# Image stage of a ViT tower with experts: attention heads doubled in round mode products, and a new order of the stage's work

## The chip, the cores and the metric

One core of a Trainium2 chip runs the whole program. The metric is the device time in microseconds (us) of one execution. Engines are named as in the profile: PE is TensorE's matmul and PEld its weight load, DVE is VectorE, ACT is ScalarE, POOL is GpSimd, SP is SyncE, which only issues DMAs here.

## The reference, cut to what matters

The input is 32 images of 3x256x256. Each becomes 256 tokens of 256 numbers (gray value, two Scharr filters, sum of absolute values), a class token is put in front, and an attention block and a layer of routed experts follow. The change touches the attention of the image rows alone:

```python
x_proj = jax.nn.silu(x @ W1 + b1)
u, v, q, k = jnp.split(x_proj, 4, axis=-1)          # 16 heads of 16 channels
scores = jnp.einsum("bqhd,bkhd->bhqk", qh, kh)
attn = jax.nn.silu(scores) / S
av = jnp.einsum("bhqk,bkhd->bqhd", attn, vh).reshape(B, S, D)
y = _layernorm(av * u, gamma, beta) @ W2 + b2
```

All data are float32.

## The kernel before, in words

The program has an image stage, a class stage, a router and an expert stage. The image stage is the subject here. It is one block in which each engine runs its own list of instructions; `steps` (L458) calls each engine's `body(n, r)` for n from -3 to 33, fully unrolled. A step works on five images at once, in a software pipeline: a = n+2 (edges, norm), b = n+1 (projections q, k, u, v), c = n (scores, silu, weighted sums), d = n-1 (gate, norm z, W2, residual h2, norm xf), e = n-2 (statistics of the rows and the router's first product). Gray images are made at gm = n+3 (L230 to L243). The order inside a step is written out by hand for each engine: PE at L619 to L669, ACT at L724 to L780, DVE at L844 to L913, POOL at L923, SP at L951. Engines meet in semaphores, so an instruction that waits holds all that is behind it on its engine.

PE's small results (all but scores and weighted sums) share two PSUM banks in turn: `UNITS` (L465) lists the 14 uses of a step, and `bank_free` (L473) makes a use wait until the use two places before it has been read (`READ`, L468). The four score products of an image write ps_s, which ACT must have read before the next (L557), and the weighted sums write ps_av.

Two kinds of matmul occur. Plain float32 operands (marked f32 and two records for each call in the trace): scores (`score`, L554), weighted sums (`weighted`, L565), edge filters (`conv`, L495), class scores (`cls_scores`, L536). Round mode operands (fp32r, one record for each call), where a value is split into a rounded part and a rest and multiplied three times (`mm3`, L198): the projections and W2. Heads have 16 channels, and a tile of the array has 32 rows. So ACT writes k twice in `silu_k` (L698), once with the odd heads' channels scaled to zero and once with the even heads' (four activations of 128x256), and a product over 32 rows of q and such a k gives one head. `score` issues 8 calls for each of its four parts, on four row tiles j.

```python
last = nc.tensor.matmul(ps_s[j // 2][:, j % 2, kt, :], k2[r % 2][32 * j:32 * j + 32, e, a, kt * 128:kt * 128 + 128],
                        q2[r % 2][32 * j:32 * j + 32, a, :], start=True, stop=True)
```

Of the kernel before, what the change touches and what calls it, by code (L numbers as in the profile page):

```python
# [18 lines left out]
P = 128  # L19
# [43 lines left out]
CE2 = CQM + 8  # L63
CLV = CE2 + 2
# [6 lines left out]
def constants(nb):  # L71
# [15 lines left out]
    for j in range(4):  # L87
        for par in range(2):
            c[32 * j + 16 * par:32 * j + 16 * par + 16, CQM + 4 * par + j] = 1
            c[32 * j + 16 * par:32 * j + 16 * par + 16, CE2 + par] = 1  # L90
# [26 lines left out]
def build(nc, x, cls_rows, w1, b1uv, b1qk, w2, b2, gb, taps, r1w, r1s, r1m, r1b, r2w, wexp, consts, out,  # L117
# [9 lines left out]
    with ctx:  # L127
# [42 lines left out]
        bk4 = s1("bk4", [P, 4])  # L170
# [97 lines left out]
        with nc.Block() as block:  # L268
# [42 lines left out]
            def _(dve):  # L311
# [48 lines left out]
                for a in range(2):  # L360
                    nc.vector.tensor_scalar(cw[:, a, :], cst[:, CMK:CMK + 32], qkcf[:, 2 + a, 0:1], None, ALU.mult)
                    nc.vector.tensor_scalar(cw[:, 2 + a, 0:8], cst[:, CQM:CQM + 8], qkcf[:, a, 0:1], None, ALU.mult)
                    nc.vector.tensor_scalar(bk4[:, 2 * a:2 * a + 2], b1qk_sb[:, 2:4], cst[:, CE2 + a:CE2 + a + 1], None, ALU.mult)
# [60 lines left out]
        q2 = [s1(f"q2{i}", [P, 2, D]) for i in range(2)]  # L424
        k2 = [s1(f"k2{i}", [P, 2, 2, D]) for i in range(2)]
# [15 lines left out]
        stat_a, ve_a, rs_a, xn_done, xt_ps, xt_hi, xt_done = (sem(n) for n in ("stat_a", "ve_a", "rs_a", "xn_done", "xt_ps", "xt_hi", "xt_done"))  # L441
        qk_ps, qk_act, uv_ps, uv_sum, uv_act = (sem(n) for n in ("qk_ps", "qk_act", "uv_ps", "uv_sum", "uv_act"))
# [15 lines left out]
        def steps(eng, body):  # L458


            for n in range(-3, NB + 2):
# [3 lines left out]
        UNITS = ["B0", "A0", "E", "D0", "D1", "G0", "B1", "D2", "A1", "D3", "B2", "B3", "B4", "D4"]  # L465
        LAG = {"E": 0, "G": -2, "D": -1, "B": 1, "A": 2}
# [4 lines left out]
                "B3": (uv_sum, 2, 1), "B4": (uv_sum, 2, 2), "D4": (xft_done, 1, 1)}  # L471
# [22 lines left out]
        def _(pe):  # L494
# [33 lines left out]
            def proj_uv(n, m, hf, unit):  # L528
                bank_free(pe, n, unit)
                for kt in range(2):  # L530
# [5 lines left out]
            def cls_scores(n, r, m):  # L536

                bank_free(pe, n, "E")
                for a in range(2):
                    nc.tensor.matmul(bank("E")[32 * a:32 * a + 32, 0:R], cw[:, a, :], q2[r % 2][:, a, :], start=True, stop=True)  # L540
# [6 lines left out]
            def cls_turn(m):  # L547

                mine = ps_av[1][:, 320:448].rearrange("p (c k) -> p k c", k=2)
# [4 lines left out]
            def score(n, r, m, t):  # L554
                if t == 0:
                    pe.wait_ge(qk_act, 2 * m + 2)
                wait(pe, attn, 8 * m + 2 * t)  # L557
                e, a = t // 2, t % 2
                for kt in range(2):
                    for j in range(4):  # L560
                        last = nc.tensor.matmul(ps_s[j // 2][:, j % 2, kt, :], k2[r % 2][32 * j:32 * j + 32, e, a, kt * 128:kt * 128 + 128],  # L561
                                                q2[r % 2][32 * j:32 * j + 32, a, :], start=True, stop=True)
# [56 lines left out]
            def body(n, r):  # L619
                a, b, c, d, e = n + 2, n + 1, n, n - 1, n - 2  # L620
                if has(b):
# [3 lines left out]
                if has(a):  # L625
                    conv(n, r, a, 0, "A0")
                if has(c):
                    cls_scores(n, r, c)
                    score(n, r, c, 1)
                    pe.wait_ge(cls_act, c + 1)  # L630
                    wait(pe, av_out, 4 * c)
                if has(d):
                    back(n, r, d, 0)
                if has(c):
                    cls_turn(c)
                if has(d):
                    back(n, r, d, 1)
                if has(e):
                    stats_turn(n, e)
                if has(b):  # L640
                    proj_qk(n, b, 0, "B1")
                if has(e):
                    router_pre(n, e)
                if has(c):
                    weighted(n, r, c, 0)
                if has(d):
                    transposes(n, "D2", z, z_done, d + 1, zt_ps)
                if has(c):
                    score(n, r, c, 2)
                if has(a):  # L650
                    conv(n, r, a, 1, "A1")
                if has(d):
                    proj_out(n, d)
                if has(c):
                    weighted(n, r, c, 1)
                if has(b):
                    proj_qk(n, b, 1, "B2")
                if has(c):
                    score(n, r, c, 3)
                if has(b):  # L660
                    proj_uv(n, b, 0, "B3")
                if has(c):
                    weighted(n, r, c, 2)
                if has(b):
                    proj_uv(n, b, 1, "B4")
                if has(d):
                    transposes(n, "D4", xf, xf_done, d + 1, xft_ps)
# [6 lines left out]
        def _(act):  # L674
            def body(n, r):
                a, b, c, d, e, gm = n + 2, n + 1, n, n - 1, n - 2, n + 3
# [14 lines left out]
                def silu_q():  # L691
                    act.wait_ge(qk_ps, 2 * b + 1)
                    for t in range(2):
                        last = nc.scalar.activation(q2[(r + 1) % 2][:, t, :], bank("B1")[:, 256 * t:256 * t + 256], ACT.Silu,
# [3 lines left out]
                def silu_k():  # L698
                    act.wait_ge(qk_ps, 2 * b + 2)
                    for t in range(2):  # L700
# [3 lines left out]
                    last.then_inc(qk_act, 1)  # L704

# [17 lines left out]

                if has(b):  # L724
                    turned_hi(xt, "B0", xt_ps, uv_ps, 2 * b, b, xt_hi)
                if has(c):
                    silu_scores(0)
                if has(a):
                    abs_edges(0)
                if has(c):  # L730
                    act.wait_ge(cls_ps, c + 1)
                    wait(act, clt_ps, c)
                    wait(act, cls_ready, c)
                    wait(act, avt_ps, 2 * (c - 1))
                    nc.scalar.activation(clf[:, :], bank("E")[:, 0:R], ACT.Silu)
                    nc.scalar.activation(cls_s[r % 2][:, :], bank("E")[0:64, 0:R], ACT.Silu).then_inc(cls_act, 1)
                    silu_scores(1)
                    act.wait_ge(clt_ps, c + 1)
                    wait(act, av_ps, 4 * c)
                    nc.scalar.activation(at[:, :, :, :, R].rearrange("p (e a) j k -> p e a (j k)", a=2),  # L740
                                         ps_av[1][:, 320:448].rearrange("p (a e x) -> p e a x", a=2, e=8)[:, 0:2, :, :], ACT.Copy).then_inc(clt_out, 1)
                if has(e):
                    act.wait_ge(st_ps, e + 1)
                    wait(act, r1_ps, e)
                    nc.scalar.activation(stt[:, :], bank("G0")[0:96, 256:512], ACT.Copy).then_inc(st_hi, 1)
                if grayed(gm):
                    gray_red(act, gm)
# [1179 lines left out]
```

## Time and profile before

| | before |
|---|---|
| median of 3 runs | 1576.35 us (1574.7 to 1579.21) |
| the profiled execution, its own time | 1575.64 us |
| its span in the profile | 1573.9 us |
| mean granted PE clock over the span | 0.924 of full speed |
| PE busy, share of the span | 1357.2 us, 86% |
| DVE busy | 1042.5 us, 66% |
| ACT busy | 904.5 us, 57% |
| POOL busy | 418.8 us, 27% |

The span runs from the first to the last instruction on the core, and 1.7 us of the execution's own time lie outside it. Busy shares are averages over stages with different limits. A row of the timeline gives the start in us, the duration in us, engine, line, operation, output and inputs, shapes, the count of merged instructions, and in brackets how long the engine sat idle before it and who released it. A duration contains the latency of the pipeline; how often instructions can follow each other is read from their starts.

### The profile page before, as it was taken

Reading aid. Unit: us, or ns where it says so; the run is one execution under the profiler, and the core shown is the slowest. Engines: PE = TensorE matmul, PEld = TensorE weight load, DVE = VectorE, ACT = ScalarE, POOL = GpSimd, SP = SyncE. Lnnn points to the kernel's source line nnn. Section 1 sums busy time; section 2 is a strip of 40 time slices with the busy share of each in tenths; the row PEclk is TensorE's granted clock in tenths of the full one; section 3 lists DMA queues with packets and bytes.
Section 4 is the critical chain, followed back from the end, with each engine's and each line's share of the span. In section 5 each row is a group of like instructions: output and inputs, shape, how many; then the busy total and the mean of one; then the engine's idle time right before and its main releaser. Section 6 shows DMA issues by size and latency. Waiting matters only on the chain. (4 is left out here: it accounts for less than half of the span.)

```text
span 1573.9 us, 32849 instructions
## 1 busy us (share of the span) xinstructions
PE 1357.2 (86%) x12092; PEld 1063.4 (68%) x12092; DVE 1042.5 (66%) x2696; ACT 904.5 (57%) x1628; POOL 418.8 (27%) x434
## 2 busy tenths in 40 slices
PE   3899999999999999999984723339999999999996
PEld 1566666666666666666653713229999999999996
DVE  4356666566666666666644487887777777777774
ACT  1577777777777777777762215344455555455552
POOL 0112212122121221212201000013555554545553
PEclk8899999999999999999996555579999999999999
DMA  7324435334243342443203330005565655556552
GB/s 225 100 77 120 119 82 133 102 99 132 76 126 108 93 133 80 121 113 88 65 28 108 114 3 0 1 9 186 145 193 150 185 167 169 172 164 184 151 162 26
DMA packets 128869, 177.33 MB, mean 113 GB/s; under 512 B 19994, under 2 KB 117164, under 8 KB 124652
## 3 DMA queue, kind: packets, MB, share of 16 engines
q1 hardware_dynamic: 111340, 154.45, 32.5%
q0 software_dynamic: 17408, 21.25, 8.4%
q8 instruction: 78, 1.28, 0.3%
q14 instruction: 43, 0.35, 0.1%
HBM read 134.24 MB, written 41.41 MB: 112 GB/s over the span
## 5 line engine op out<-in xcount | busy, mean ns | idle before, releaser
L682 ACT ACTIVATE at<-ps_s 128x1024 f32<-128x1024 f32 x256 | 248.8, 1028 | 42.7 <-PE ps_s L561 42.7
L202 PE MATMUL ps_s<-xet,whi 128*128 128x322 f32 x640 | 205.7, 321 | 12.4 <-issue 10.9
L1869 POOL DMA_INDIRECT out_rows<-ye,slot_token x96 | 153.4, 1598 | 225.4 <-ACT ye L1714 215.0
L203 PE MATMUL ps_s<-xet,wlo 128*128 128x322 f32 x640 | 199.9, 312 | 0.0
L204 PE MATMUL ps_s<-xet,whi 128*128 128x322 f32 x640 | 198.7, 311 | 0.0
L1683 ACT ACTIVATE sg<-ps_s 128x322 f32<-128x322 f32 x160 | 70.4, 440 | 176.8 <-PE ps_s L204 126.0
L1784 DVE TENSOR_TENSOR wlo<-raw,whi 128x640 fp32r<-128x640 f32 x192 | 154.0, 818 | 2.3 <-ACT whi L1693 1.3
L561 PE MATMUL ps_s<-q,k 32*128 32x256 f32 x2048 | 146.6, 400 | 1.4 <-ACT at L682 1.4
L577 PE MATMUL ps_av<-at,uv 128*16 128x257 f32 x2048 | 136.0, 383 | 0.3 <-ACT at L740 0.3
L202 PEld LDWEIGHTS ps_s<-xet,whi 128*128 128x128 f32 x640 | 121.3, 190 | 20.6 <-issue 20.0
L202 PE MATMUL ps_av<-whi,hs 128*128 128x256 f32 (+1 forms) x480 | 134.4, 280 | 0.8 <-DVE wlo L1784 0.5
L204 PE MATMUL ps_av<-wlo,hs 128*128 128x256 f32 (+1 forms) x480 | 134.4, 280 | 0.0
L203 PE MATMUL ps_av<-whi,hs 128*128 128x256 f32 (+1 forms) x480 | 134.4, 280 | 0.0
L1767 DVE TENSOR_TENSOR hm<-ps_s,sg 128x322 f32<-128x322 f32 x128 | 63.2, 494 | 99.9 <-ACT sg L1683 80.9
L921 POOL TENSOR_TENSOR rsz<-vez,n 128x2 f32<-128x2 f32 x32 | 30.9, 967 | 354.9 <-DVE vez L802 354.9
L204 PEld LDWEIGHTS ps_s<-xet,whi 128*128 128x128 f32 x640 | 121.5, 190 | 0.0
L203 PEld LDWEIGHTS ps_s<-xet,wlo 128*128 128x128 f32 x640 | 121.3, 190 | 0.0
L561 PEld LDWEIGHTS ps_s<-q,k 32*128 32x128 f32 x2048 | 92.5, 184 | 33.2 <-ACT at L682 14.8
L1853 POOL DMA_INDIRECT xe<-token_rows,slot_token x96 | 102.5, 1068 | 30.2 <-issue 28.7
L1693 ACT ACTIVATE whi<-raw 128x640 fp32r<-128x640 f32 x128 | 93.0, 731 | 11.9 <-PEq L1511 11.9
L202 PE MATMUL ps_f<-xt,w1s 128*128 128x256 f32 x256 | 78.8, 308 | 10.6 <-DVE y L826 9.2
L921 POOL TENSOR_TENSOR rsh<-veh,n 128x2 f32<-128x2 f32 x32 | 23.3, 728 | 234.0 <-DVE veh L802 234.0
(357 smaller groups left out, 3367.8 us busy)
## 6 DMA issues: line engine op xcount, KB each, us to landing
raw<-in_wexp SPq DMA_DIRECT2D x32, 1280.0 KB, 6.3
halo<-gray_dram SPq DMA_DIRECT2D x96, 288.0 KB
xb<-in_x SPq DMA_DIRECT2D x64, 384.0 KB, 5.1
raw<-in_wexp SPq DMA_DIRECT2D x32, 640.0 KB
gray_dram<-g SPq DMA_DIRECT2D x32, 256.0 KB, 3.2
out_rows<-h SPq DMA_DIRECT2D x64, 128.0 KB, 6.8
token_rows<-xf SPq DMA_DIRECT2D x64, 128.0 KB, 4.2
pre_dram<-pre SPq DMA_DIRECT2D x32, 128.0 KB, 5.1
```

Source lines behind the costliest of these rows:

```text
L202: nc.tensor.matmul(o, lh, rh, start=first, stop=False)
L203: nc.tensor.matmul(o, ll, rh, start=False, stop=False)
L204: return nc.tensor.matmul(o, lh, rl, start=False, stop=last)
L561: last = nc.tensor.matmul(ps_s[j // 2][:, j % 2, kt, :], k2[r % 2][32 * j:32 * j + 32, e, a, kt * 128:kt * 128 + 128], q2[r % 2][32 * j:32 ...
L577: last = nc.tensor.matmul(o[32 * j:32 * j + 16, 0:R + 1], uv[r % 2][:, kt, 256 + h * 16:256 + h * 16 + 16], at[:, t, j, kt, 0:R + 1], star ...
L682: nc.scalar.activation(at[:, t, 2 * i:2 * i + 2, :, 0:R].rearrange("p j k q -> p (j k) q"), ps_s[i][:, :, :, :].rearrange("p j k q -> p (j ...
L1683: nc.scalar.activation(sg[b][:, :], ps_s[b][:, 0, :, :].rearrange("p k q -> p (k q)")[:, 0:CW], ACT.Silu).then_inc(gate_act, 1)
L1693: nc.scalar.activation(whi[r][:, lo:hi], raw[r][:, lo:hi], ACT.Copy).then_inc(w_hi_up, 1)
L1767: nc.vector.tensor_tensor(hm[b][:, :], o, sg[b][:, :], ALU.mult).then_inc(h_done, 1)
L1784: nc.vector.tensor_tensor(wlo[r][:, lo:hi], raw[r][:, lo:hi], whi[r][:, lo:hi].bitcast(f32), ALU.subtract).then_inc(done, 1)
L1853: nc.gpsimd.indirect_dma_start(out=xe[r][0:w, st, :], out_offset=None, in_=token_rows, in_offset=bass.IndirectOffsetOnAxis(ap=slot_token[0 ...
L1869: nc.gpsimd.indirect_dma_start(out=out, out_offset=bass.IndirectOffsetOnAxis(ap=slot_token[0:w, 3 * m + st:3 * m + st + 1], axis=0), in_=y ...
```

## The change

- Scores: q and k are kept once (qn, kn). A new DVE `stream_shuffle` copies them into dup, where each group of 32 rows holds the same 16 channels twice, one copy for the even and one for the odd heads. From it q becomes a rounded part (ACT, `hi_q`) and a rest (DVE, `split_q`), and k becomes one tile whose upper 16 rows hold the rounded part and whose lower 16 hold the rest (DVE, `stack_k`). A product is then two round mode calls, with q's rounded part and q's rest, in place of one float32 call of two records.
- `cls_scores` reads qn and kn: 4 calls in place of 6. `silu_k` has 2 activations in place of 4.
- Gray images are made at gm = n+4, and the halo load on SP waits for the edge filters of the image that used the buffer.
- The turn of xf and the row statistics move from image d at the end of a step to image e within the next (unit D4 becomes F0). All engines get a new order.
- POOL computes the inverse root of norm a ahead of that of norm h. SP stores pre after h2.

```diff
-        UNITS = ["B0", "A0", "E", "D0", "D1", "G0", "B1", "D2", "A1", "D3", "B2", "B3", "B4", "D4"]
+        UNITS = ["A0", "B0", "D0", "D1", "E", "F0", "B1", "B2", "D2", "B3", "A1", "D3", "G0", "B4"]
@@ cls_scores
-                for e in range(2):
-                    for a in range(2):
-                        last = nc.tensor.matmul(bank("E")[64 + 32 * a:96 + 32 * a, 0:R], cw[:, 2 + a, :], k2[r % 2][:, e, a, :],
-                                                start=e == 0, stop=e == 1)
+                for a in range(2):
+                    last = nc.tensor.matmul(bank("E")[64 + 32 * a:96 + 32 * a, 0:R], cw[:, 2 + a, :], kn[:, a, :], start=True, stop=True)
@@ score
-                    pe.wait_ge(qk_act, 2 * m + 2)
+                    pe.wait_ge(q_ready, m + 1)
+                    pe.wait_ge(k_ready, m + 1)
...
+                    for hl in range(2):
+                        for j in range(4):
+                            row = slice(32 * j, 32 * j + 32)
+                            last = nc.tensor.matmul(ps_s[j // 2][:, j % 2, kt, :], kd[r % 2][row, e, a, kt * 128:kt * 128 + 128],
+                                                    qd[r % 2][row, hl, e, a, :], start=hl == 0, stop=hl == 1)
@@ silu_k
-                        for par in range(2):
-                            last = nc.scalar.activation(k2[(r + 1) % 2][:, par, t, :], bank("B2")[:, 256 * t:256 * t + 256], ACT.Silu,
-                                                        bias=bk4[:, 2 * par + t:2 * par + t + 1], scale=cst[:, CE2 + par:CE2 + par + 1])
+                        last = nc.scalar.activation(kn[:, t, :], bank("B2")[:, 256 * t:256 * t + 256], ACT.Silu,
+                                                    bias=b1qk_sb[:, 2 + t:3 + t])
@@ new on ACT
+                def hi_q():
+                    act.wait_ge(q_dup, b + 1)
+                    wait(act, scores, 4 * (b - 1))
+                    nc.scalar.activation(qd[(r + 1) % 2][:, 0, :, :, :].rearrange("p e t q -> p (e t q)"),
+                                         dup[:, :, :, :].rearrange("p e t q -> p (e t q)"), ACT.Copy).then_inc(q_hi, 1)
@@ new on DVE
+                def shuffled(src, ready, done):
+                    dve.wait_ge(qk_act, ready)
+                    nc.vector.memset(spare[:, :], 0.0)
+                    for par in range(2):
+                        half = [16 * par + i for i in range(16)]
+                        last = nc.vector.stream_shuffle(dup[:, par, :, :].rearrange("p t q -> p (t q)"),
+                                                        src[:, :, :].rearrange("p t q -> p (t q)"), half + half)
+                    last.then_inc(done, 1)
...
+                def split_q():
+                    dve.wait_ge(q_hi, b + 1)
+                    nc.vector.tensor_tensor(qd[(r + 1) % 2][:, 1, :, :, :].rearrange("p e t q -> p (e t q)"),
+                                            dup[:, :, :, :].rearrange("p e t q -> p (e t q)"),
...
+                def stack_k():
...
+                    dve.wait_ge(k_dup, b + 1)
+                    nc.vector.tensor_copy(flat_k, flat_d).then_inc(k_hi, 1)
+                    dve.wait_ge(k_hi, b + 1)
+                    nc.vector.scalar_tensor_tensor(flat_k, flat_k.bitcast(f32), cst[:, CUP:CUP + 1], flat_d,
+                                                   ALU.mult, ALU.add).then_inc(k_ready, 1)
@@ sync
                 if grayed(gm):
+                    sp.wait_ge(conv_done, 2 * (gm - 1))
                     load_halo(sp, gm)
```

The orders of a full step, by the names of the units and functions:

```
PE before   B0 score0 A0 E score1 D0 turn D1 G0(statistics) B1 G0(router) weighted0 D2 score2 A1 D3 weighted1 B2 score3 B3 weighted2 B4 D4 weighted3
PE after    A0 B0 score0 D0 D1 E F0 score1 turn B1 B2 D2 score2 B3 A1 D3 G0(statistics) weighted0 weighted1 score3 B4 weighted2 G0(router) weighted3
ACT after   abs(A0) hi(B0) gray_red silu0 class_silu hi(F0) silu1 silu_q silu_k hi(D2) hi_q abs_rows abs(A1) class_column silu2
            stats_hi av_copy0 silu3 av_copy1 silu_uv0 keep_pre av_copy2 silu_uv1 av_copy3
DVE after   lo(B0) most gated0 gated1 stats_z gray_green lo(F0) class_lo edges0 norm_z gray_blue double_q lo(D2) least biased0 last_stats
            edges1 split_q residual stats_a stats_h stats_lo double_k biased1 norm_a stack_k norm_f keep_class
```

## Rows read from the trace of the kernel before

**Rows 1.** Page, part 2: busy tenths in 40 slices, and granted clock

```profile
PE   3899999999999999999984723339999999999996
...
PEclk8899999999999999999996555579999999999999
```

**Rows 2.** Windows: busy us (instructions) by engine, then granted clock, DMA share, GB/s

```profile
400.00:500.00 100.00, 98.53 (x1030) 63.91 (x1026) 62.81 (x195) 74.01 (x131) 19.86 (x28) 1.00 0.38 105
...
760.00:980.00 220.00, 128.84 (x953) 99.03 (x951) 130.26 (x335) 90.04 (x142) 14.71 (x26) 0.68 0.21 49
980.00:1574.00 594.00, 513.48 (x3737) 500.46 (x3737) 447.84 (x945) 284.76 (x544) 256.52 (x194) 0.93 0.49 137
```

**Rows 3.** All instructions on the tile q, whole trace: first and last start

```profile
L561 PE MATMUL ps_s<-q,k x2048: 374/374/478, 58.8 to 825.3; 32*128 32x256 f32 x187
```

**Rows 4.** Timeline of PE, one step's pieces that the sum uses

```profile
402.58 0.38 PE L202 MATMUL ps_f<-xt,w1s 128*128 128x256 f32 x1 [0.30 <-DVE y L826]
...
406.63 1.15 PE L561 MATMUL ps_s<-q,k 32*128 32x256 f32 x16
407.70 1.07 PE L502 MATMUL ps_f<-halo,band 108*32 108x256 f32 x16
408.71 0.38 PE L202 MATMUL ps_f<-w2s,zt 128*128 128x256 f32 x1
...
421.18 1.07 PE L502 MATMUL ps_f<-halo,band 108*32 108x256 f32 x16
422.31 0.41 PE L540 MATMUL ps_f<-q,cw 128*32 128x256 f32 x2
...
423.31 1.15 PE L561 MATMUL ps_s<-q,k 32*128 32x256 f32 x16
...
430.46 0.66 PE L512 MATMUL ps_f<-cst,z 128*128 128x128 f32 x4
431.05 1.15 PE L561 MATMUL ps_s<-q,k 32*128 32x256 f32 x16
```

**Rows 5.** Timeline of PE, windows that cut one product after four, eight and twelve records

```profile
406.63 0.50 PE L561 MATMUL ps_s<-q,k 32*128 32x256 f32 x4
...
406.63 0.71 PE L561 MATMUL ps_s<-q,k 32*128 32x256 f32 x8
...
406.63 0.93 PE L561 MATMUL ps_s<-q,k 32*128 32x256 f32 x12
```

**Rows 6.** Timeline of PE: round mode calls on the whole array follow each other

```profile
402.81 0.28 PE L203 MATMUL ps_f<-xt,w1s 128*128 128x256 f32 x1
...
403.05 0.28 PE L202 MATMUL ps_f<-xt,w1s 128*128 128x256 f32 x1
```

**Rows 7.** Groups by shape, 100 to 700 us: busy, mean ns | idle before, releaser

```profile
L702 ACT ACTIVATE k<-ps_f,bk,cst 128x256 f32<-128x256 f32 x96 | 46.3, 563 | 27.5 <-PE ps_f L204 27.5
...
L694 ACT ACTIVATE q<-ps_f,b1qk_sb 128x256 f32<-128x256 f32 x50 | 20.9, 469 | 26.4 <-PE ps_f L204 26.4
...
L233 ACT ACTIVATE g<-xb 128x512 f32<-128x512 f32 x25 | 15.5, 619 | 0.0
```

**Rows 8.** Groups by shape, 740 to 1574 us: wider instructions on ACT and DVE

```profile
L1693 ACT ACTIVATE whi<-raw 128x640 fp32r<-128x640 f32 x128 | 93.0, 731 | 11.9 <-PEq L1511 11.9
...
L1471 DVE TENSOR_TENSOR shared<-ps_s,shared 128x1024 f32<-128x1024 f32 x2 | 2.4, 1220 | 0.6 <-PE ps_s L1350 0.6
```

**Rows 9.** Timeline of DVE: two instructions of 512 elements follow each other

```profile
419.26 0.69 DVE L812 TENSOR_TENSOR xft<-ps_f,xft 128x512 fp32r<-128x512 f32 x1 [0.37 <-ACT xft L722]
419.87 0.68 DVE L898 TENSOR_REDUCE stats<-xf 128x2 f32<-128x512 f32 x1
```

**Rows 10.** Groups of DVE by shape, 0 to 40 us

```profile
L325 DVE CAST w1s<-stage 128x2048 fp32r<-128x2048 f32 x1 | 1.2, 1228 | 0.0
...
L337 DVE CAST w2s<-stage 128x512 fp32r<-128x512 f32 x1 | 0.4, 419 | 0.0
```

**Rows 11.** Waits in 100 to 700 us: who waited for whom, us, times, longest

```profile
DVE h L871 <- PE ps_f L204: 56.5, 24, 2.4
```

More of the change, by code:

```diff
@@ L706, in silu_uv, with keep_pre, abs_rows @@
+                def keep_pre():
+                    act.wait_ge(r1_ps, e + 1)
+                    wait(act, pre_out, 16 * e)
+                    nc.scalar.activation(pre[:, :], bank("G0")[:, 0:256], ACT.Copy).then_inc(pre_done, 1)
+                def abs_rows():
+                    act.wait_ge(xf_done, e + 1)
+                    wait(act, st_done, e)
+                    nc.scalar.activation(axf[:, :, :], xf[:, :, :], ACT.Abs).then_inc(axf_done, 1)
                 def silu_uv(hf):
@@ L730, in body @@
+                if has(e):
+                    turned_hi(xft, "F0", xft_ps, r1_ps, e, e, xft_hi)
                 if has(c):
[L731 to L736, printed above, removed]
@@ L737, in body @@
-                    silu_scores(1)
[L738 to L745, printed above, removed]
@@ L746, in body @@
-                if grayed(gm):
-                    gray_red(act, gm)
+                    silu_scores(1)
                 if has(b):
                     silu_q()
-                if has(e):
-                    act.wait_ge(r1_ps, e + 1)
-                    wait(act, pre_out, 16 * e)
-                    nc.scalar.activation(pre[:, :], bank("G0")[:, 0:256], ACT.Copy).then_inc(pre_done, 1)
-                if has(c):
-                    av_copy(0)
+                    silu_k()
                 if has(d):
@@ L757, in body @@
                     turned_hi(zt, "D2", zt_ps, w2_ps, d, d, zt_hi)
-                if has(c):
-                    silu_scores(2)
+                if has(b):
+                    hi_q()
+                if has(e):
+                    abs_rows()
                 if has(a):
@@ new lines, in body @@
+                if has(b):
+                    turned_lo(xt, bank("B0")[:, :], xt_hi, b, xt_done)
+                if has(e):
+                    most()
+                if has(d):
+                    gated(0)
+                    gated(1)
+                    stats_z()
+                if grayed(gm):
+                    gray_green(dve, gm)
+                if has(e):
+                    turned_lo(xft, bank("F0")[:, :], xft_hi, e, xft_done)
+                if has(c):
+                    class_lo()
@@ new lines, in body @@
+                if has(a):
+                    edges(0)
+                if has(d):
+                    norm_z()
+                if grayed(gm):
+                    gray_blue(dve, gm)
+                if has(b):
+                    double_q()
+                if has(d):
+                    turned_lo(zt, bank("D2")[:, :], zt_hi, d, zt_done)
+                if has(e):
+                    least()
+                if has(b):
+                    biased(0)
+                if has(e):
+                    last_stats()
@@ new lines, in body @@
+                if has(a):
+                    edges(1)
+                if has(b):
+                    split_q()
+                if has(d):
+                    residual()
+                if has(a):
+                    stats_a()
+                if has(d):
+                    stats_h()
+                if has(e):
+                    stats_lo()
+                if has(b):
+                    double_k()
+                    biased(1)
+                if has(a):
+                    norm_a()
@@ L915, in _ @@
+                if has(b):
+                    stack_k()
+                if has(d):
+                    norm_f()
+                if has(c):
+                    keep_class()
             steps(dve, body)
```

218 lines of the change are left out of this document (116 added, 102 removed).

## The prediction

> **What bounds the kernel now.** I read the page first: in the first half of the span nearly every slice shows PE at nine tenths or more, at full clock [rows 1]. The windows come next. From 100 to 700 us six windows look alike, of which one stands here: PE busy for 98.5 of 100 us at clock 1.00, ACT for 74, DVE for 63 and POOL for 20 [rows 2]. So the image stage is bound by PE's own work. The two windows from 760 us on hold the last four images, then the class, router and expert stages, which the change doesn't touch [rows 2]. The 2048 score records begin at 58.8 and end at 825.3 us, in 32 steps [rows 3]. One step lasts from 406.63 to 431.05, which is 24.42 us [rows 4]. Whatever PE work the change takes out of a step counts 32 times, as long as DVE, which has 37 idle us in 100, takes what it is given.
>
> **Scores on PE.** A product of 16 float32 records takes 1.07 us, from 406.63 to the next unit at 407.70 [rows 4]. Windows that cut it show 0.50 us after four records, then 0.71 and 0.93: four row tiles work side by side, and each further four cost 0.22 us [rows 5]. A round mode call with the same 256 columns on the whole array follows the one before after 0.12 us (402.81 to 403.05 for two), weight load included [rows 6]. The new product has the same 16 records in four groups of four. If the groups follow each other in 0.11 us instead of 0.22, it takes 1.07 - 4 x 0.107 = 0.64 us. The trace shows no round mode call on row tiles. Its lower bound is a group per 0.11 us, its upper bound the float32 group of 0.22, and I take the lower, since operand type and columns are those of [rows 6] and the tiles overlap already in [rows 5]. Gain: 4 x 0.43 = 1.72 us in a step.
>
> **Class scores on PE.** They take 1.00 us (422.31 to 423.31) [rows 4] and have k twice. Two of six calls go, so each of the two k tiles has two records less, and they run one behind the other: 2 x 0.22 = 0.43 us gained, bounds 0.2 (by the call count alone a third, 0.33) and 0.45.
>
> **Waits of PE that go.** In a step PE waits 0.30 us at B1 for the gate's y, and the conv unit at 421.18 takes 1.13 us where the one at 407.70 takes 1.01, because the class scores wait for xt's rest: 0.42 us together [rows 4]. The new order puts B1 five units behind y. I count 17 passages between row tiles, column tiles and the whole array in either order, so nothing is won or lost there; putting weighted 0 and 1 in a row only undoes what moving A0 away from the class scores does. Without any wait the step is 24.42 - 1.72 - 0.43 - 0.42 = 21.85 us.
>
> **Waits that come.** D1 needs the bank of B0, so xt's rest. I place the chain A0, B0, ACT's abs and rounding (0.6 each, as its copy of 512 [rows 7]), DVE's rest (0.7 [rows 9]), each with about 0.1 us of handing over: xt is ready some 3.2 us into the step, just when PE reaches D1 (A0 1.0 and B0 0.6, as the conv unit and the turn of z take [rows 4], score0 0.65, D0 an estimated 0.9). The class scores then need gated0, which on DVE stands behind xt's rest and `most`: 0.1 to 0.2 us late. Everything later has room in my reckoning of the step: xf's rest is there 0.6 us ahead of B2, biased0 at 12.9 for D3 at 13.0, the statistics 0.6 us ahead of G0, k 0.9 us ahead of the next scores. With biased0 that close I leave 0.45 us of waits in all: **22.3 us a step**, with 21.9 and 22.8 as the bounds of this case.
>
> **ACT.** `silu_k` falls from four activations of 563 ns to two of 469 [rows 7]: -1.3 us. `hi_q` copies 1024 columns from SBUF; by the copies of 512 in 619 ns [rows 7] and of 640 in 731 [rows 8] that is 0.88 ns a column, so 1.07 us. ACT stays at 18 us in a step, 81% of 22.3. `hi_q` stands ahead of abs_rows, abs(A1) and silu2, which A1's readers and score3 wait for; silu2 ends near 16.1 us and score3 starts near 17, so it is covered. Without that cover it would cost its 1.07 us.
>
> **DVE.** Busy 62.8 in 100 us [rows 2] is 15.3 us in a step. Instructions of 512 elements follow each other in 0.61 us [rows 9]. Added: four shuffles of 512 (4 x 0.61 = 2.4; no row has one; the bounds are the two-elements-a-cycle cast of 512, 0.42 [rows 10], and, as nothing slower is near, twice the row, 1.2; I take 0.61 as for every other two-operand or reduce instruction of this size), `split_q` and the last part of `stack_k` on 1024 elements (1.22 each, as the tensor_tensor [rows 8]), the rounding copy (0.69, between 512 in 419 and 2048 in 1228 ns [rows 10]), two memsets and four waits on its own results (0.4). That is 5.9, so 21.2 us of 22.3. It moves into time in which DVE waits for PE, for D3 above all (56.5 us in 24 steps [rows 11]), so the place is there, but DVE is now nearly as full as PE. The Trainium skill (VectorE: DVE Perf Modes, "The perf-mode tier table") has `STREAM_SHUFFLE` at one element a cycle, about 2400 ns for 2048; by it the four cost 0.7 us each at most, and the sum would not move. What is queued behind the new waits: double_q waits for silu_q with lo(D2), least and biased0 behind it; it is free 0.2 us before silu_q ends.
>
> **POOL and SP.** The swapped roots change no work; norm a now comes first, as DVE asks. The halo load waits for A1, about 13 us in, with the stores of h2 (ready at 16), pre (21.6) and xf (23.9) behind it: none is late. The buffer is filled a step earlier than it is read. The gray images only start one step sooner.
>
> **Start and end.** For the first image, q and k pass DVE between projection and score: shuffles, rounding copy, last part, 1.2 + 0.7 + 1.2 us, uncovered: +3. In the last steps the extra DVE work of image e lies ahead of image d's chain: +1.
>
> **The sum.** (24.42 - 22.3) x 32 = 68 us less, 4 us more: 64 us. From the profiled execution's 1575.64 this gives 1511.6; the median of 1576.35 lies 0.7 above it, so 1512.
>
> **The rivals.**
> - *DVE sets the pace* (13%). If shuffles come with extra instructions, or the waits for own results are longer, the 21.2 us grow, and since DVE and PE wait for each other at D1, E, D2 and D3, waits add up. At 23.4 us a step: 1.0 x 32 - 4 = 29 us less, 1547. For it: only 1 us of room. Against it: every wait I placed ends before its user.
> - *The narrow products do not halve* (10%). If a group on row tiles still takes 0.22 us, the step is 24.0 us and the time 1575.6 - 13 + 4 = 1567. Something in between would come of a least time for each record. Against that, a record now costs 0.22 / 4 = 0.054 us [rows 5]. The Trainium skill (TensorE: Matmul & The Clock Gate, "Wait — 56ns, not 53.3ns?") speaks against this change: it has about 62 ns of sequencer time for each MATMUL where hardware decoding is off. By it a product would take 0.99 us and not 0.64, the step 23.7 us and the time 1557. The 0.054 us of [rows 5] lie below that figure, so I give this form 4 of the 10%.
> - *The shuffles are slow* (8%, the case on the slower side). DVE's sum passes the present 24.42 us when a shuffle takes more than 0.61 + 3.2 / 4 = 1.4 us. At 1.75 us the step is 25.8 us: 1.35 x 32 + 4 = 47 us more, 1623. Against it: the instructions of this size on DVE take 0.42 to 0.69 us, whatever they do [rows 9, 10].
>
> **How the numbers follow.** The forecast has 69%: 1499 (21.9 us a step) to 1528 (22.8). The range goes from 1499 to 1556, which takes in the rival in which DVE sets the pace and leaves out about two in ten. A measurement of this kernel tells 0.3% (4.7 us) from no change. Faster: the forecast, DVE's pace and nearly all of the narrow products, 88%. Same: the part of the second and third cases in which little is left of the gain, 4%. Slower: 8%.
>
> **What would show it.** Right: groups of four records in score 0.11 us apart, a product in 0.64 us; 22.3 us from score0 to score0; PE busy for 97 to 98% in the steady stretch, DVE for 93 to 96%; shuffles of 0.69 us. Wrong: PE's busy share near 90% with waits for DVE (the second case), products of 1 us (the third), shuffles over 1.4 us (the last), or a granted clock below 1.00 in the stage.

## The result, and the profile after (the changed kernel is 4.2% faster)

| | before | after |
|---|---|---|
| median, each of 4 runs on one chip | 1576.84 us (1574.7 to 1579.21) | 1509.98 us (1507.63 to 1512.37) |
| the profiled execution, its own time | 1575.64 us | 1509.77 us |
| its span | 1573.9 us | 1508.0 us |
| PE busy, share of the span | 1357.2 us, 86% | 1299.1 us, 86% |
| DVE busy | 1042.5 us, 66% | 1203.6 us, 80% |

The ratio is 0.9576, with a 95% interval of 0.9555 to 0.9596. The forecast was 1512 us.

The page of the changed kernel, busy time, PE's slices and the granted clock (against [rows 1]):

```profile
PE 1299.1 (86%) x11964; PEld 1047.3 (69%) x11964; DVE 1203.6 (80%) x3110; ACT 894.2 (59%) x1596; POOL 439.7 (29%) x434
...
PE   3799999999999999999958133369999999999996
...
PEclk8799999999999999999965555689999999999999
```

Its windows: one from the middle of the image stage, then two that start 68 us earlier than those of [rows 2]:

```profile
400.00:500.00 100.00, 99.84 (x1141) 67.56 (x1142) 93.02 (x280) 79.33 (x141) 28.77 (x34) 1.00 0.49 128
692.00:912.00 220.00, 131.97 (x1009) 102.39 (x1001) 148.65 (x385) 93.33 (x149) 19.51 (x32) 0.66 0.23 52
912.00:1508.00 596.00, 515.01 (x3737) 501.63 (x3737) 448.00 (x945) 285.59 (x546) 254.45 (x194) 0.93 0.48 136
```

PE is now busy for 99.8 of 100 us where it was for 98.5, and DVE for 93 where it was for 63. Behind the image stage PE's busy time is nearly that of before (132 and 515 us against 129 and 513). So the gain lies in the image stage. The records of the score products, in the view by tile (against [rows 3]):

```profile
L569 PE MATMUL ps_s<-qd,kd x2048: 268/277/578, 62.6 to 757.5; 32*128 32x256 f32 x187
```

The first one comes 3.8 us later than before (62.6 against 58.8) and the last one 67.8 us earlier (757.5 against 825.3). What follows it up to the end of the span takes 750.5 us, where it took 748.6. The three add up: 3.8 - 71.6 + 1.9 = -65.9 us, which is the difference of the spans.

The first image's way, in the timeline of PE, and the first distance from score0 to score0 in a window (the kernel before has 58.80 to 78.40 us there, at clock 1.00):

```profile
60.60 1.12 PE L514 MATMUL ps_f<-cst,xn 128*128 128x128 f32 x4 [3.42 <-DVE xn L827]
62.61 1.23 PE L569 MATMUL ps_s<-qd,kd 32*128 32x256 f32 x16 [0.90 <-DVE kd L899]
```

```profile
62.60:83.80 21.20, 19.04 (x210) 12.71 (x210) 11.95 (x30) 14.68 (x25) 1.95 (x2) 0.82 0.37 92
```

PE waits 3.42 us for DVE's norm and 0.90 us for k. Behind that the granted clock averages 0.82 (0.50 up to 70.0 us), and this distance is 21.2 us where it was 19.6. PE is idle for 2.2 us of it, where it was idle for 1.2 before.

The timeline of PE, the pieces of one step (against [rows 4]); the full step runs from 413.51 to 435.52:

```profile
404.91 1.93 PE L585 MATMUL ps_av<-at,uv 128*16 128x257 f32 x32
406.77 0.75 PE L569 MATMUL ps_s<-qd,kd 32*128 32x256 f32 x16
407.45 0.50 PE L201 MATMUL ps_f<-w1s,xt 128*128 128x512 f32 x1
...
413.51 0.75 PE L569 MATMUL ps_s<-qd,kd 32*128 32x256 f32 x16
414.19 0.49 PE L595 MATMUL ps_f<-vc,cls_s 64*128 64x512 f32 x1
...
416.20 0.41 PE L545 MATMUL ps_f<-qn,cw 128*32 128x256 f32 x2
...
416.46 0.39 PE L547 MATMUL ps_f<-kn,cw 128*32 128x256 f32 x2
416.88 0.63 PE L514 MATMUL ps_f<-cst,xf 128*128 128x128 f32 x4
...
435.52 0.74 PE L569 MATMUL ps_s<-qd,kd 32*128 32x256 f32 x16
```

A product takes 0.68 us to the next unit (406.77 to 407.45, 413.51 to 414.19), where it took 1.07. The class scores take 0.68 (416.20 to 416.88), where they took 1.00. No row of this stretch has a wait of PE in brackets, but rows show brackets only from 0.15 us on, and starts show a shorter wait. It lies at F0 (416.88). F0 takes the bank of D1, two places on, so it needs DVE's second half of the gate, which ends at 416.73:

```profile
416.31 0.42 DVE L848 TENSOR_TENSOR y<-ps_f,uv 128x256 f32<-128x256 f32 x1 [0.40 <-PE ps_f L598]
```

In products_only (below), where a score product stands behind the same class scores, they take 0.57 us. The unit behind makes no difference by itself: the old class scores take 1.00 us ahead of a product (before) and ahead of F0 (order_only). So 0.11 us of the 0.68 is this wait. The step is 22.01 us here; over the whole trace the median distance from one score0 to the next is 22.04, against 24.43 before. Windows that cut the product after four, eight and twelve records (against [rows 5]):

```profile
413.51 0.39 PE L569 MATMUL ps_s<-qd,kd 32*128 32x256 f32 x4
...
413.51 0.52 PE L569 MATMUL ps_s<-qd,kd 32*128 32x256 f32 x8
...
413.51 0.63 PE L569 MATMUL ps_s<-qd,kd 32*128 32x256 f32 x12
```

Each further group of four round mode records adds about 0.12 us, where a float32 group added 0.22. DVE's and ACT's new instructions, groups by shape from 100 to 700 us:

```profile
L874 DVE STREAM_SHUFFLE dup<-kn 128x512 f32<-128x512 f32 x56 | 39.2, 748 | 0.0
...
L874 DVE STREAM_SHUFFLE dup<-qn 128x512 f32<-128x512 f32 x54 | 37.4, 739 | 0.0
L899 DVE SCALAR_TENSOR_TENSOR kd<-kd,cst,dup 128x1024 fp32r<-128x1024 f32 x28 | 36.0, 1285 | 1.0
L884 DVE TENSOR_TENSOR qd<-dup,qd 128x1024 fp32r<-128x1024 f32 x27 | 32.9, 1218 | 0.0
...
L897 DVE CAST kd<-dup 128x1024 fp32r<-128x1024 f32 x28 | 19.1, 683 | 0.0
...
L874 DVE LOAD_MASK_SELECT dup<-qn x54 | 0.3, 6 | 0.0
L714 ACT ACTIVATE qd<-dup 128x1024 fp32r<-128x1024 f32 x27 | 28.8, 1068 | 0.0
L707 ACT ACTIVATE kn<-ps_f,b1qk_sb 128x256 f32<-128x256 f32 x54 | 22.6, 470 | 15.6 <-PE ps_f L203 15.6
```

A shuffle lasts 739 to 748 ns; in the timeline the second starts 0.63 us after the first. It comes with an instruction that loads the mask, which takes 6 ns.

### The profile page after: what moved, and what is told of

Its sections match the earlier page's. It is cut to its first block and busy times, and to the rows that moved or that the text cites. A ratio compares the mean times of both kernels' runs of the same rounds, so it can differ in the third digit from the quotient of the medians.

```text
span 1508.0 us, 33286 instructions
## 1 busy us (share of the span) xinstructions
PE 1299.1 (86%) x11964; PEld 1047.3 (69%) x11964; DVE 1203.6 (80%) x3110; ACT 894.2 (59%) x1596; POOL 439.7 (29%) x434
## 5 line engine op out<-in xcount | busy, mean ns | idle before, releaser
L201 PEld LDWEIGHTS ps_s<-xet,whi 128*128 128x128 f32 x640 | 121.7, 190 | 20.5 <-issue 19.9
L585 PE MATMUL ps_av<-at,uv 128*16 128x257 f32 x2048 | 130.6, 385 | 1.2 <-ACT at L728 0.8
L1024 POOL TENSOR_TENSOR rsa<-vea,n 128x2 f32<-128x2 f32 x32 | 22.1, 691 | 356.9 <-DVE vea L823 356.9
L569 PE MATMUL ps_s<-qd,kd 32*128 32x256 f32 x2048 | 96.5, 305 | 3.3 <-issue 1.3
L569 PEld LDWEIGHTS ps_s<-qd,kd 32*128 32x128 f32 x2048 | 70.1, 186 | 34.6 <-issue 31.7
L585 PEld LDWEIGHTS ps_av<-at,uv 128*16 128x16 f32 x2048 | 50.4, 97 | 56.5 <-issue 19.0
L1820 ACT ACTIVATE ye<-ps_av,weight 128x256 f32<-128x256 f32 (+1 forms) x96 | 45.3, 473 | 72.5 <-PE ps_av L203 71.0
```

Source lines behind the costliest of these rows:

```text
L201: nc.tensor.matmul(o, lh, rh, start=first, stop=False)
L569: last = nc.tensor.matmul(ps_s[j // 2][:, j % 2, kt, :], kd[r % 2][row, e, a, kt * 128:kt * 128 + 128], qd[r % 2][row, hl, e, a, :], start ...
L585: last = nc.tensor.matmul(o[32 * j:32 * j + 16, 0:R + 1], uv[r % 2][:, kt, 256 + h * 16:256 + h * 16 + 16], at[:, t, j, kt, 0:R + 1], star ...
```

## The experiments

All steps below are medians over a trace of the distance from score0 to score0. An ordinary repetition of the changed kernel stands first, as the measure for all that edit it.

**changed_again.** The changed kernel, unedited.

> The changed kernel as it is, as the yardstick on this chip for the three kernels sent with it: 1510 us by its first measurement, within 0.2%.

Measured: 1508.28 us (1507.86 to 1509.73, 5 runs), ratio 0.957 (0.9557 to 0.9583), step 22.02 us. The two medians of this kernel differ by 0.1%.

### What the products bring

**f32_products.** The changed kernel with the same tiles and the same work on DVE and ACT, but float32 operands and one call where two were. The rest of q is made and not read; k's tile holds the full k where it had the rounded part, and zeros for the rest.

```diff
-        qd = [s1(f"qd{i}", [P, 2, 2, 2, D], f32r) for i in range(2)]
-        kd = [s1(f"kd{i}", [P, 2, 2, D], f32r) for i in range(2)]
+        qd = [s1(f"qd{i}", [P, 2, 2, 2, D]) for i in range(2)]
+        kd = [s1(f"kd{i}", [P, 2, 2, D]) for i in range(2)]
-                    for hl in range(2):
-                        for j in range(4):
+                    for j in range(4):
...
-                                                    qd[r % 2][row, hl, e, a, :], start=hl == 0, stop=hl == 1)
+                                                qd[r % 2][row, 0, e, a, :], start=True, stop=True)
```

> The changed kernel, all DVE and ACT work kept, but the doubled q and k are float32 and a product is one float32 call (8 calls of two records). Theory PE (PE's own work sets the step, DVE has room): a product goes from 0.68 back to about 1.07 us, 4 x 0.39 = 1.56 us a step, step 23.6 us, time 1510 + 50 = 1560 us. Rival DVE (DVE at 93% sets the step): the step hardly moves, 1510 to 1520 us.

Measured: 1555.98 us (1555.1 to 1556.77, 4 runs), ratio 0.9867 (0.985 to 0.9883), step 23.60 us. Its window:

```profile
400.00:500.00 100.00, 99.84 (x1051) 66.59 (x1051) 87.30 (x259) 74.50 (x132) 24.84 (x28) 1.00 0.43 116
```

PE is as full as in the changed kernel. The operand type alone (with half as many calls of the same 16 records) is worth 23.60 - 22.04 = 1.56 us a step, which is 4 x 0.39, and 46 us in all. DVE has the same work in both kernels. If it set the changed kernel's step, the step would have grown by less than the products did; it grew by all of it.

**products_only.** The new products with the old order of all engines. `hi_q` stands ahead of av_copy1 on ACT, and on DVE double_q behind lo(D2), split_q and double_k behind norm_f, stack_k ahead of biased1.

```diff
-        UNITS = ["A0", "B0", "D0", "D1", "E", "F0", "B1", "B2", "D2", "B3", "A1", "D3", "G0", "B4"]
+        UNITS = ["B0", "A0", "E", "D0", "D1", "G0", "B1", "D2", "A1", "D3", "B2", "B3", "B4", "D4"]
```

> The order of before with the new products: double_q behind the rest of zt, split_q and double_k ahead of biased0, stack_k ahead of biased1, hi_q behind abs(A1). If the products' gain needs no new order: step 24.42 - 1.56 - 0.32 = 22.54 us plus the late start, 1520 us. Theory (the order carries it): k is ready about 0.7 us after score0 wants it and the rest of xt, behind k's work and the statistics on DVE, comes some 2 us late, which gives the whole gain back: 24 to 25 us a step, 1565 to 1595 us.

Measured: 1622.53 us (1622.22 to 1622.99, 4 runs), ratio 1.0289 (1.0271 to 1.0306), step 25.57 us. Its timeline of PE and its window:

```profile
413.45 0.63 PE L514 MATMUL ps_f<-cst,xn 128*128 128x128 f32 x4 [1.54 <-DVE uvp L850]
...
416.86 0.41 PE L543 MATMUL ps_f<-qn,cw 128*32 128x256 f32 x2 [1.11 <-DVE xt L827]
...
417.43 0.74 PE L565 MATMUL ps_s<-qd,kd 32*128 32x256 f32 x16
...
420.89 0.39 PE L201 MATMUL ps_f<-xt,w1s 128*128 128x256 f32 x1 [0.30 <-DVE y L841]
...
410.69 0.69 DVE L880 CAST kd<-dup 128x1024 fp32r<-128x1024 f32 x1
411.42 1.28 DVE L882 SCALAR_TENSOR_TENSOR kd<-kd,cst,dup 128x1024 fp32r<-128x1024 f32 x1
412.62 0.68 DVE L850 TENSOR_TENSOR uvp<-ps_f,b1uv_sb 128x512 f32<-128x512 f32 x1
...
416.12 0.68 DVE L827 TENSOR_TENSOR xt<-ps_f,xt 128x512 fp32r<-128x512 f32 x1
```

```profile
400.00:500.00 100.00, 87.43 (x964) 57.25 (x960) 82.13 (x241) 70.41 (x122) 22.23 (x28) 1.00 0.40 105
```

This is slower than the 24 to 25 us a step that I had expected. PE has less work than before but waits three times for DVE, 2.95 us a step; with shorter waits it is idle for 12.6 in 100 us, which is 3.2 us a step. The first wait is for the second half of the biased u and v (uvp), which DVE reads out of its bank from 412.62 on, behind the two parts of stack_k (410.69 to 412.70); B0, two places on, needs that bank. The second is for xt's rest (416.12), behind the row statistics. DVE is busy for only 82%: it isn't full, its work stands in the wrong place. The class scores take 0.57 us to the next product here (416.86 to 417.43), 0.43 less than before the change.

**order_only.** The other half: the new order with the old float32 products, no shuffles, and `silu_k` with its four activations.

```diff
-                        last = nc.scalar.activation(kn[:, t, :], bank("B2")[:, 256 * t:256 * t + 256], ACT.Silu,
-                                                    bias=b1qk_sb[:, 2 + t:3 + t])
+                        for par in range(2):
+                            last = nc.scalar.activation(k2[(r + 1) % 2][:, par, t, :], bank("B2")[:, 256 * t:256 * t + 256], ACT.Silu,
+                                                        bias=bk4[:, 2 * par + t:2 * par + t + 1], scale=cst[:, CE2 + par:CE2 + par + 1])
...
-                if has(b):
-                    hi_q()
```

> The changed kernel's order of all engines, with the products, silu_k and class scores of before (no shuffles, no hi_q, split_q, stack_k). Theory PE: the 0.42 us of waits that the new order removes and some 0.15 us of tile changes: step 24.42 - 0.57 = 23.85 us, 1558 us. Rival (the order only serves the heavier DVE and is worth nothing by itself): 24.4 us a step, 1576 us. If DVE sets the changed kernel's step, this one, with 6 us less on DVE, would fall to near 1510 or below.

Measured: 1583.24 us (1582.53 to 1584.23, 5 runs), ratio 1.0037 (1.0023 to 1.0051), step 24.56 us, where I had expected 23.85. I had missed a wait. The timelines of PE and of ACT:

```profile
412.03 0.50 PE L202 MATMUL ps_f<-w1s,xt 128*128 128x512 f32 x1 [0.51 <-ACT k L701]
...
410.05 1.93 ACT L701 ACTIVATE k<-ps_f,bk,cst 128x256 f32<-128x256 f32 x4 [0.58 <-PE ps_f L204]
```

B3 takes the bank of k, two places on. Four activations take 1.93 us (410.05 to 411.98), and PE stands at B3 until they end. The next experiment takes that cause away.

**order_only_half_k.** order_only with two of the four activations: half of k (par 1) is left out, its place holds zeros that POOL wrote once. The scores of half the heads are missing from the output.

```diff
-                        for par in range(2):
+                        for par in range(1):
                             last = nc.scalar.activation(k2[(r + 1) % 2][:, par, t, :], ...
```

> order_only with two of silu_k's four activations left out (k2 for the odd heads stays zero, so half of the scores are left out of the result's meaning, not of PE's work). In order_only PE waits 0.51 us at B3 for silu_k of 1.93 us, which in the new order follows B2 at once. Theory: with silu_k at 0.9 us the wait goes: step 24.56 - 0.6 = 23.95 us, 1583 - 20 = 1563 us. Rival (the wait at B3 is replaced by another, behind zt or biased0): step 24.3 to 24.5 us, 1575 to 1583 us.

Measured: 1564.78 us (1563.63 to 1565.93, 4 runs), ratio 0.9917 (0.9902 to 0.9932), step 24.00 us, and PE is busy throughout:

```profile
400.00:500.00 100.00, 100.00 (x1052) 66.59 (x1055) 62.21 (x195) 69.57 (x125) 19.36 (x28) 1.00 0.43 114
```

So the four activations cost order_only 0.56 us a step. Without them the new order is worth 24.43 - 24.00 = 0.43 us a step, the 0.42 of waits that [rows 4] show, and nothing beside them.

### Whether DVE has room

**dve_plus_1.** The changed kernel with one more reduction over 768 elements on DVE in each step, ahead of norm_f; nothing reads its output.

```diff
+                if has(c):
+                    for i in range(1):
+                        nc.vector.tensor_reduce(xtra[:, i:i + 1], cst[:, 0:768], AX.X, ALU.max)
                 if has(d):
                     norm_f()
```

> The changed kernel with one more reduce of 768 elements (about 0.86 us) on DVE in each step, ahead of norm_f; nobody reads its result. Theory PE (DVE has about 1.4 us of room in a step): at most 0.1 us a step shows, 1510 to 1513 us. Rival DVE: all 0.86 us show, 1510 + 27 = 1537 us.

Measured: 1514.57 us (1513.09 to 1519.45, 4 runs), ratio 0.9615 (0.9597 to 0.9633), step 22.24 us. Of the 0.86 us by which each reduction holds DVE, 0.20 shows, twice what I had expected at most. It shows at D1, which waits for xt's rest:

```profile
417.44 0.66 PE L599 MATMUL ps_f<-cst,avs 128*128 128x128 f32 x4
418.24 0.50 PE L596 MATMUL ps_f<-vc,cls_s 64*128 64x512 f32 x1
```

D1 starts 0.80 us behind the turn before it, where the changed kernel has 0.58 (414.61 to 415.19). The room in front of D1 is about 0.66 us.

**dve_plus_3.** The same with three of them (`range(3)`).

> The changed kernel with three reduces of 768 elements (2.6 us) more on DVE in each step. dve_plus_1 showed 0.20 of its 0.86 us, so DVE has about 0.66 us of room; if DVE sets the pace from there on, 2.6 - 0.66 = 1.9 us show: step 23.95 us, 1510 + 61 = 1570 us. Rival (my first figure of 1.4 us of room): step 23.2 us, 1548 us. If waits between DVE and PE add up beyond the sum: over 24.2 us, above 1578 us.

Measured: 1589.21 us (1588.93 to 1591.05, 4 runs), ratio 1.0072 (1.0056 to 1.0087), step 23.97 us. The step is the one expected and the time 19 us above. The median step hides why: seven of the 31 distances are 26.5 to 28.5 us long. A step of the common kind and a long one behind it, then pieces of that one, in windows; the wait of PE in the long step; and the score product at 387.64:

```profile
358.00:382.00 24.00, 22.12 (x257) 15.05 (x257) 22.97 (x65) 17.66 (x32) 5.47 (x7) 1.00 0.42 109
382.00:408.90 26.90, 25.02 (x257) 17.68 (x253) 23.03 (x65) 17.70 (x32) 5.46 (x7) 0.87 0.39 99
...
385.00:387.00 2.00, 1.68 (x14) 0.82 (x14) 1.71 (x5) 0.00 (x0) 0.00 (x0) 1.00 0.40 131
...
389.00:391.00 2.00, 2.00 (x10) 1.88 (x10) 2.00 (x6) 1.86 (x2) 0.25 (x1) 0.50 0.00 0
...
393.00:395.00 2.00, 2.00 (x16) 1.83 (x16) 1.44 (x5) 0.44 (x3) 0.00 (x0) 0.71 0.73 136
```

```profile
385.28 0.50 PE L596 MATMUL ps_f<-vc,cls_s 64*128 64x512 f32 x1 [1.84 <-DVE xt L834]
...
387.64 1.23 PE L570 MATMUL ps_s<-qd,kd 32*128 32x256 f32 x16
```

In every step PE waits some 1.85 us at D1 for xt's rest, which DVE now makes late. In seven of them the granted clock falls behind that wait to 0.50, the lower of its two levels (1.2 GHz, not 2.4). In five it is back at 1.00 after 7 us, in the other two after 10. In the step shown the product lasts 1.23 us and not 0.75, and the step costs 2.9 us more; the seven cost 2.5 to 4.5 us each and 22 us together, which covers the 19 us above the expectation. Products_only has four long steps, of 28.3 to 28.9 us, some 12 us more together; the one from 593.1 us, seen in a window, has a granted clock of 0.82. Order_only, with its wait of 0.5 us, has none. That the waits bring the clock down is read from this order of events and from these four kernels (the changed one, without long waits, has no long step either); no run moved a wait to test it.

### What the order of PE's units is worth

**gray_3_ahead.** The gray images made one step later again, as in the kernel before.

```diff
-a, b, c, d, e, gm = n + 2, n + 1, n, n - 1, n - 2, n + 4
+a, b, c, d, e, gm = n + 2, n + 1, n, n - 1, n - 2, n + 3
```

> The changed kernel with gray images made at n+3 again in place of n+4. Theory PE: the halo is stored and loaded some 4 us ahead of its use in any case, nothing changes but the start by a few tenths of a us: within 2 us of the changed kernel. Rival (the earlier gray is needed, since the halo load now waits behind A1 or is late for A0, now the first unit of the step): 0.5 to 1 us a step, 1525 to 1540 us.

Measured: 1509.71 us (1506.5 to 1511.34, 5 runs), ratio 0.9572 (0.9559 to 0.9585), step 22.06 us. The step ahead is worth nothing that can be told.

**weighted_apart.** The first weighted sum ahead of the turn of the statistics, so that the two are no longer in a row.

```diff
+                if has(c):
+                    weighted(n, r, c, 0)
                 if has(e):
                     stats_turn(n, e)
                 if has(c):
-                    weighted(n, r, c, 0)
                     weighted(n, r, c, 1)
```

> The changed kernel with weighted0 ahead of the statistics' turn, so that weighted0 and weighted1 no longer follow each other: two more passages between column tiles and the whole array. Theory: a passage costs PE time by itself; the pair took 1.86 us against 2 x 1.0 apart, so 0.15 us a step, 5 us slower than the changed kernel (1515). Rival (a passage costs nothing, or the wait structure hides it): same time.

Measured: 1516.57 us (1516.29 to 1519.27, 5 runs), ratio 0.9627 (0.9614 to 0.964), step 22.29 us: 0.27 more, for two more passages between narrow output tiles and wide ones.

**router_first.** The same edit in the other direction: the router's product ahead of weighted2, so that weighted2 and weighted3 are in a row too.

```diff
+                if has(e):
+                    router_pre(n, e)
                 if has(c):
                     weighted(n, r, c, 2)
-                if has(e):
-                    router_pre(n, e)
-                if has(c):
                     weighted(n, r, c, 3)
```

> The changed kernel with the router's product ahead of weighted2, so that weighted2, weighted3 and the next step's A0 stand in a row: two passages less. Theory PE: 0.15 us a step less, 1510 - 5 = 1505 us, as DVE's statistics are there 1.8 us before. Rival DVE (DVE sets the pace or is met at once): no gain, 1510 us; or weighted3 waits for silu3 and av_copy1, up to 0.5 us a step, 1520 us.

Measured: 1504.69 us (1503.09 to 1505.21, 5 runs), ratio 0.9543 (0.953 to 0.9556), step 21.80 us, against 1508.28 and 22.02 in changed_again. Its timeline of PE has the two as one row:

```profile
406.00 0.49 PE L201 MATMUL ps_f<-w1s,xt 128*128 128x512 f32 x1
...
408.40 1.93 PE L585 MATMUL ps_av<-at,uv 128*16 128x257 f32 x32
410.15 1.05 PE L504 MATMUL ps_f<-halo,band 108*32 108x256 f32 x16
```

From B4 to A0, the stretch that the edit touches, PE now needs 4.15 us (406.00 to 410.15) where the changed kernel needs 4.49 (407.45 to 411.94). The step gains less than this 0.34. From B0 to score0 it takes 0.68 us (411.13 to 411.81) where it took 0.59, and k's last part ends only at 411.70. Weighted_apart has its 0.27 without such a wait: its window from 400 to 500 us has PE busy for 99.84 of 100 us. So one passage is worth 0.13 to 0.17 us on PE, and of the 0.34 that two of them free, 0.22 reaches the step. The Trainium skill (TensorEngine Tiling (Array Packing), "Key Properties") says that changing the tiling mode drains the engine, and gives no time for it. These steps agree with it in that each passage costs time, and they put a price to it; no row shows the drain itself.

**class_first.** router_first with the class scores directly behind A0, since both write narrow tiles, to save two more passages; on ACT class_silu stands ahead of hi(B0).

```diff
-        UNITS = ["A0", "B0", "D0", "D1", "E", "F0", ...
+        UNITS = ["A0", "E", "B0", "D0", "D1", "F0", ...
```

> The kernel router_first with the class scores right behind A0 (both on column tiles), their silu on ACT behind abs(A0), gray_red behind silu0: two more passages less. Theory PE: weighted_apart priced a pair of passages at 0.28 us, so 21.80 - 0.28 = 21.5 us a step, 9 us under router_first: 1496 us. Rival (DVE, with 0.66 us of room by dve_plus_1 and 0.24 already used, is met): 21.6 to 21.8 us a step, 1499 to 1505 us.

Measured: 1508.15 us (1506.62 to 1508.37, 5 runs), ratio 0.9556 (0.9543 to 0.9569), step 22.03 us. A miss: 0.23 us a step worse than router_first. Its timeline of PE, and one row of its weight loads:

```profile
413.57 0.63 PE L514 MATMUL ps_f<-cst,xn 128*128 128x128 f32 x4 [0.38 <-ACT edge L690]
...
419.88 0.39 PE L201 MATMUL ps_f<-xt,w1s 128*128 128x256 f32 x1
```

```profile
419.88 0.19 PEld L201 LDWEIGHTS ps_f<-xt,w1s 128*128 128x128 f32 x1 [0.20 <-DVE xft L833]
```

B0 is now two places behind A0 and must wait for ACT's absolute values of A0, 0.38 us in each step. That takes back what the passages give: from A0 to score1 it is 5.54 us here (411.72 to 417.26) and 5.59 in router_first (410.15 to 415.74). The loss lies behind it. B1 and B2 take 3.21 us (418.21 to 421.42) where they took 2.96 (416.68 to 419.64), because B2, at 419.88, waits for DVE's rest of xf in the bank of F0, which ends at 419.82. With the class scores moved ahead of B0, PE comes to B2 some 0.9 us sooner behind B0, and DVE's rest of xf only 0.1 (5.57 us behind B0, for 5.69). So the bank rule is met twice, once with ACT and once with DVE.

## Why the prediction was right

The time was 1509.98 us for a forecast of 1512, and the likeliest case came true. But the sum met the time by terms that were off in both directions, and part of the closeness is luck: the steps gave 8.5 us more than forecast, and the start and the end took back 6.6.

| | forecast | measured |
|---|---|---|
| step before - step after | 24.42 - 22.3 = 2.1 us | 24.43 - 22.04 = 2.39 us |
| that, 32 times | 68 us | 76.5 us |
| start and end | 4 us more | 76.5 - 65.9 = 10.6 us more |
| sum | 64 us less | 65.9 us less (spans) |

By its steps:

- **What bounds the kernel.** Right. What the change takes from PE's list shows in full, and PE's share went from 98.5 to 99.8%.
- **Scores.** The bound that I took, round mode groups at the pace of the whole array, is right: 0.12 us a group. But "0.64 us" was 0.68 and the gain 4 x 0.39 = 1.56 us, not 1.72; f32_products shows the same 1.56. The row that I took the pace from had 0.12 us a call, and the term took half of the float32 interval, 0.107, in its place. Each of the four groups gave 0.10 us of it and not 0.107 (0.43 in a product against 0.39).
- **Class scores.** Right in size, 0.43 us: products_only has 0.57 us where it was 1.00. In the new order only 0.32 is left of it, since F0 behind them waits.
- **Waits that go.** Right, 0.42 forecast, 0.43 measured with order_only_half_k. The count of passages ("nothing is won or lost") holds too, in sum.
- **Waits that come.** Mis-sized, and in the change's favour. I had left 0.45 us and 0.11 came, at F0 for the second half of the gate, while I had placed 0.1 to 0.2 us at the class scores for the first half. D1 does not wait: xt's rest ends at 414.98 and D1 starts at 415.19. For the next scores k is done 0.36 us ahead, and not 0.9. The terms as measured are 1.56 + 0.43 + 0.43 - 0.11 = 2.31 us of the 2.39 by which the step fell. Of the other 0.08, 0.03 lies at F0's own turn (0.56 for 0.59 us in order_only_half_k) and 0.03 at the router's product (0.79 for 0.82), both without a reason in the rows. The scores' gain was too large by 0.16 and the waits by 0.34, so the step is 22.04 where I said 22.3.
- **ACT.** Right where it was tested: `hi_q` takes 1068 ns for the forecast 1.07 us, and ACT is busy for 79% against my 81. What I missed is that the shorter `silu_k` (two activations, 0.9 us of ACT) is no mere saving on an idle engine. It is what keeps B3 from waiting; without it the new order costs time (order_only).
- **DVE.** The pace of a shuffle is 0.63 us for my 0.61, the parts on 1024 elements 1218, 1285 and 683 ns for 1.22, 1.22 and 0.69. DVE is busy for 20.5 us of a step (93.02% of 22.04); my 21.2 had 0.4 us of waits in it. Room in front of D1: 0.66 us by dve_plus_1, where I said "only 1 us".
- **Start, end.** Mis-sized: 10.6 us where I had 3 + 1. The first score comes 3.8 us late, for a forecast of 3. The next distance grew by 1.6 us instead of falling by 2.4, which is 4.0 us. PE is idle for 1.0 us more in it, and its row has a likely reason for the rest that I had not thought of: behind the new waits of the start PE runs at a mean clock of 0.82, where it ran at 1.00. The thirty distances behind it fell by 72.9 us together, 1.2 more than thirty times 2.39. From the last score0 to the end it takes 1.6 us more instead of 2.4 less, 4.0 us again. There, too, the clock is low earlier than before: in a window from 749.0 to 757.5 us, ahead of the last scores, it is 0.60, while the kernel before has 1.00 from 800 us on to its last scores at 825.3. How much of these last 4.0 us is the clock and how much DVE's longer chain, which I had put at 1, no run takes apart.

The rivals: the narrow products do nearly halve (0.12 us a group for 0.22). The Trainium skill's rule that spoke against them (TensorE: Matmul & The Clock Gate, "Wait — 56ns, not 53.3ns?", about 62 ns for each MATMUL where hardware decoding is off) does not describe this case: four records in 0.117 us are 29 ns each. No run shows whether hardware decoding was on. Shuffles at 0.63 us are far from the 1.4 at which the sign turns. That DVE sets the pace was the nearest to coming true: one reduction of 0.86 us already shows by a quarter, three make the kernel slower than the one before, and in the old order DVE holds PE up while it is busy for 82%.

The two parts don't add up. Steps in us:

| | old products | new products |
|---|---|---|
| old order | 24.43 | 25.57 |
| new order | 24.56 (24.00 with half of k) | 22.04 |

These are medians, so the four long steps of products_only are not in its 25.57. The order alone is 6 us slower and the products alone 46 us slower, and together they are 67 us faster. The order gives DVE's new work places in which PE waits for it 0.11 us a step and not 2.95, and the new products shorten the activations of k, without which the order stalls at B3.

## What to carry to other kernels

When PE is full at full clock, count a change of its list unit by unit from start to start, and take the cheapest operand form that still holds the precision: here a rounded part and a rest on row tiles cost 64% of float32. Before you judge a part alone, ask which wait the other part removes; on an engine with room, the place of an instruction decides, not the sum. Keep products with the same tile shape in a row, and look at whose bank the moved unit takes, and who reads it. A wait too short for a bracket, like the 0.11 us at F0, shows only when the same unit is timed in another order.

## What the runs showed of the hardware that I had not expected

- The change between narrow and wide output tiles costs PE 0.13 to 0.17 us each time (weighted_apart, router_first), without any row that names it.
- A wait of 1.85 us in each step of an otherwise full PE went with a fall of the granted clock to 0.50 in seven of 31 steps, each time for 7 to 10 us and at a price of 2.5 to 4.5 us (dve_plus_3). With a wait of 0.5 us (order_only) it did not fall. So lateness on DVE can cost more than its own length. What decides in which steps it falls was not tried.
